# SyncE asks for the experts' first matrix two tiles ahead, in the order in which the slots come free

## The reference

```python
# layer 0: 16 experts, hidden width 512, each token goes to its 2 best
h = relu(einsum('bsh,ehf->bsef', x, w1) + b1)
expert_out = einsum('bsef,efh->bseh', h, w2) + b2
moe = sum over the token's 2 experts of topk_w * expert_out

# layer 1: 8 experts, hidden width 1024, each token goes to its 2 best
xe = xn * ln_g[e] + ln_b[e]
h = gelu(xe @ W1[e] + b1[e])
y = h @ W2[e] + b2[e]
out = sum over the token's 2 experts of weights * y
```

## Time and profile before

| | us |
|---|---|
| three runs of the kernel, median | 3487.85 |
| lowest and highest of them | 3473.99, 3497.01 |
| the profiled execution, its own time | 3479.88 |
| its span, first to last instruction | 3478.1 |
| of it, experts 0 (first hidden to last result) | 1328.4 to 1655.5 |
| of it, experts 1 (first hidden to last result) | 3022.0 to 3456.4 |

### The profile page before, as it was taken

One profiled execution on the slowest core, in us unless ns is written; L12 is line 12 of the kernel. 1 busy time (PEld: TensorE's weight loads), 2 busy tenths in 40 slices (PEclk: granted clock), 3 DMA queues, 4 the chain that ended last, 5 costly groups with the idle time before them and its releaser, 6 DMA issues. The chain is left out here.

```text
span 3478.1 us, 51218 instructions
## 1 busy us (share of the span) xinstructions
PE 2500.1 (72%) x14080; PEld 1914.7 (55%) x14080; DVE 1343.8 (39%) x4118; ACT 1441.6 (41%) x3690; POOL 2011.4 (58%) x1969
## 2 busy tenths in 40 slices
PE   0156899999999947887036666666666667499997
PEld 0123666678888836776024444444444445488986
DVE  4166889952221142000643444444444435500100
ACT  0025666647650022332354444444444443255553
POOL 0353777777777226663657777777777772033332
PEclk9998999999999958998557667666766768699998
DMA  2574766678888335565367777777777772364232
GB/s 112 191 251 126 209 202 206 206 226 257 269 257 244 123 119 186 181 208 171 104 186 203 202 198 202 202 205 204 206 203 201 205 201 61 124 179 131 37 84 62
DMA packets 314743, 620.94 MB, mean 179 GB/s; under 512 B 82206, under 2 KB 128685, under 8 KB 309777
## 3 DMA queue, kind: packets, MB, share of 16 engines
q1 hardware_dynamic: 207409, 343.11, 30.1%
q0 software_dynamic: 101360, 268.76, 29.2%
q10 hardware_dynamic: 5728, 6.11, 0.5%
HBM read 451.74 MB, written 170.90 MB: 179 GB/s over the span
## 5 line engine op out<-in xcount | busy, mean ns | idle before, releaser
L608 POOL DMA_INDIRECT agg_r_rows<-h_table,parts_and_x x856 | 869.1, 1015 | 296.1 <-issue 218.8
L657 PE MATMUL agg_r_sums<-agg_r_rows,agg_r_onehot 128*128 128x257 f32 x1712 | 703.2, 559 | 389.8 <-DVE agg_r_rows L629 343.6
L657 PEld LDWEIGHTS agg_r_sums<-agg_r_rows,agg_r_onehot 128*128 128x128 f32 x1712 | 430.4, 275 | 645.4 <-issue 581.5
L1412 POOL DMA_INDIRECT rl_buf<-r_table,kinds x608 | 634.4, 1043 | 249.3 <-issue 170.4
L629 DVE TENSOR_TENSOR agg_r_rows<-agg_r_rows,agg_r_rel 128x514 f32<-128x514 f32 x428 | 298.5, 697 | 657.6 <-DMA agg_r_rows<-h_table,parts_and_x 655.6
L575 ACT ACTIVATE agg_r_gap<-iota,parts_and_x 128x128 f32<-128x128 f32 x856 | 295.1, 392 | 496.5 <-PE agg_r_sums L657 470.9
L1782 PE MATMUL f_pH<-f_xT,f_w 128*128 128x128 f32 x2816 | 359.4, 287 | 74.5 <-DMA f_w<-in_L_ffn_w 52.9
L1782 PEld LDWEIGHTS f_pH<-f_xT,f_w 128*128 128x128 f32 x2816 | 343.8, 201 | 106.2 <-DMA f_w<-in_L_ffn_w 57.7
L1134 PE MATMUL ly_acc<-parts,matrix 128*128 128x256 bf16 x1250 | 342.0, 274 | 0.0
L1133 PE MATMUL ly_acc<-parts,matrix 128*128 128x256 bf16 x1250 | 340.2, 272 | 0.0
L1132 PE MATMUL ly_acc<-parts,matrix 128*128 128x257 bf16 (+1 forms) x1250 | 340.0, 272 | 0.0
(11 more groups left out here) (394 smaller groups left out, 3404.2 us busy)
## 6 DMA issues: line engine op xcount, KB each, us to landing
agg_r_rel<-relation_rows SPq DMA_DIRECT2D x428, 260.0 KB, 3.0
relation_rows<-rl_buf SPq DMA_DIRECT2D x304, 260.0 KB, 4.5
f_w<-in_L_ffn_W SPq DMA_DIRECT2D x28, 1024.0 KB, 5.0
f_w<-in_L_ffn_w SPq DMA_DIRECT2D x38, 512.0 KB, 5.8
relation_rows<-f_rr_buf POOLq DMA_DIRECT2D x60, 260.0 KB, 2.8
agg_r_rows<-h_table,parts_and_x POOLq DMA_INDIRECT x856, 3.4
ly_zin<-zh SPq DMA_DIRECT2D x50, 256.0 KB, 4.8
zh<-ly_out SPq DMA_DIRECT2D x50, 256.0 KB, 2.7
```

The costliest lines, as they stand in the source:

```text
L608: pool.indirect_dma_start(rows[:, n % SLOTS, t, :], None, table, bass.IndirectOffsetOnAxis(ap=indices[:, t:t + 1], axis=0)).then_inc(s_row ...
L657: last = nc.tensor.matmul(sums[:, n % BANKS, 0:used], onehot[:, n % BANKS, t, :], rows[:, n % SLOTS, t, 0:used], start=t == 0, stop=t == 1)
L1412: pool.indirect_dma_start(self.buf[:, n, g, :], None, self.table, bass.IndirectOffsetOnAxis(ap=self.c.kinds[:, at:at + 1], axis=0)).then_i ...
```

## The change

`tile` is split in three: `first(t, s)` asks for the first matrix of tile t, `second(t, s)` for the second matrix, `stored(i, s)` stores the result of tile 2i + s - 2. SP now runs first(0), first(1), second(0), first(2), second(1), first(3), and then for each tile t: second(t), the store, first(t+2). Since `first` and `second` of one call are for different tiles, each reads the expert and the flag for itself: two more table reads per tile. The waits before each DMA are the same as before.

```diff
-                def tile(i, s, stores):
-                    t = 2 * i + s
+                def first(t, s):
                     e = sp.value_load(e_tab[0:1, 0, bass.ds(t, 1)], min_val=0, max_val=ne - 1)
                     fresh = sp.value_load(e_tab[0:1, 1, bass.ds(t, 1)], min_val=0, max_val=1)
...
                     sp.wait_ge(s_h, t * HB + HB)
-                    weights(sp, fresh, w1b[:, s, :, :].rearrange("p k f -> p (k f)"), a1, s_w1[s])
+                    weights(sp, fresh, w1b[:, s, :, :].rearrange("p k f -> p (k f)"), w1[bass.ds(e, 1), :, :].rearrange("a p f -> p (a f)"), s_w1[s])
+
+                def second(t, s):
+                    e = sp.value_load(e_tab[0:1, 0, bass.ds(t, 1)], min_val=0, max_val=ne - 1)
+                    fresh = sp.value_load(e_tab[0:1, 1, bass.ds(t, 1)], min_val=0, max_val=1)
 
                     sp.wait_ge(s_y, t + 1)
-                    weights(sp, fresh, w2b[:, s, :, :].rearrange("p k f -> p (k f)"), a2, s_w2[s])
-                    if stores and out is None:
-                        sp.wait_ge(s_yb, t + 1)
-                        sp.dma_start(ys[bass.ds((i - 1) * (2 * P) + s * P, P), :], yb[:, s, :]).then_inc(s_st[s], 16)
+                    weights(sp, fresh, w2b[:, s, :, :].rearrange("p k f -> p (k f)"), w2[bass.ds(e, 1), :, :].rearrange("a p f -> p (a f)"), s_w2[s])
+
+                def stored(i, s):
+                    sp.wait_ge(s_yb, 2 * i + s + 1)
+                    sp.dma_start(ys[bass.ds((i - 1) * (2 * P) + s * P, P), :], yb[:, s, :]).then_inc(s_st[s], 16)
...
                 for s in range(2):
-                    tile(0, s, False)
-                with sp.Fori(1, tiles // 2) as i:
+                    first(s, s)
+                for s in range(2):
+                    second(s, s)
+                    first(2 + s, s)
+                with sp.Fori(1, tiles // 2 - 1) as i:
                     for s in range(2):
-                        tile(i, s, True)
+                        second(2 * i + s, s)
+                        if out is None:
+                            stored(i, s)
+                        first(2 * i + 2 + s, s)
+                for s in range(2):
+                    second(tiles - 2 + s, s)
+                    if out is None:
+                        stored(tiles // 2 - 1, s)
```

More of the change, by code:

```diff
@@ L1720, in _ @@
             def _(sp):
-                def tile(i, s, stores):
-                    t = 2 * i + s
+                def first(t, s):
                     e = sp.value_load(e_tab[0:1, 0, bass.ds(t, 1)], min_val=0, max_val=ne - 1)
                     fresh = sp.value_load(e_tab[0:1, 1, bass.ds(t, 1)], min_val=0, max_val=1)
-                    a1 = w1[bass.ds(e, 1), :, :].rearrange("a p f -> p (a f)")
-                    a2 = w2[bass.ds(e, 1), :, :].rearrange("a p f -> p (a f)")
                     sp.wait_ge(s_h, t * HB + HB)
-                    weights(sp, fresh, w1b[:, s, :, :].rearrange("p k f -> p (k f)"), a1, s_w1[s])
+                    weights(sp, fresh, w1b[:, s, :, :].rearrange("p k f -> p (k f)"), w1[bass.ds(e, 1), :, :].rearrange("a p f -> p (a f)"), s_w1[s])
+                def second(t, s):
+                    e = sp.value_load(e_tab[0:1, 0, bass.ds(t, 1)], min_val=0, max_val=ne - 1)
+                    fresh = sp.value_load(e_tab[0:1, 1, bass.ds(t, 1)], min_val=0, max_val=1)
                     sp.wait_ge(s_y, t + 1)
-                    weights(sp, fresh, w2b[:, s, :, :].rearrange("p k f -> p (k f)"), a2, s_w2[s])
-                    if stores and out is None:
-                        sp.wait_ge(s_yb, t + 1)
-                        sp.dma_start(ys[bass.ds((i - 1) * (2 * P) + s * P, P), :], yb[:, s, :]).then_inc(s_st[s], 16)
+                    weights(sp, fresh, w2b[:, s, :, :].rearrange("p k f -> p (k f)"), w2[bass.ds(e, 1), :, :].rearrange("a p f -> p (a f)"), s_w2[s])
+                def stored(i, s):
+                    sp.wait_ge(s_yb, 2 * i + s + 1)
+                    sp.dma_start(ys[bass.ds((i - 1) * (2 * P) + s * P, P), :], yb[:, s, :]).then_inc(s_st[s], 16)
                 for to, what in loads:
```

## The result

The changed kernel takes 3432.97 us (median of 4 runs, 3423.82 to 3436.64). The kernel before, run beside it, takes 3480.92 us (4 runs). The ratio is 0.9856, with a 95% interval of 0.9824 to 0.9887: 48 us less, faster by more than 1%. The profiled execution took 3435.33 us, span 3433.3; before it was 3479.88 and 3478.1, so 44.8 us of span went. 17 us were forecast.

What follows compares the result with a forecast made beforehand. PE's stalls on the first matrix cost time, but SP was to become the pace of experts 0. Gains of 9.1 us in experts 1 and 8 in experts 0 gave 3463 us profiled, 3471 on the median; range 3446 to 3508.

Steps and rivals of the forecast that it cites:

- SP's own work for a tile: Experts 0, before the change: SP's instructions take 3.4 us per tile against PE's 3.91, leaving 0.5 us to spare.
- The price of the reads: Experts 0: the second pair of table reads adds 1.35 us per tile to SP, bounds 1.1 and 1.7.
- the prediction's own chain: Experts 0: SP sets the pace at 4.75 us per tile, 59 tiles 280 us; stage ends at 1647 with crowding.
- The lead: Experts 0: SP's lead of one result and one hidden is used up at 0.8 us per tile after some six tiles.
- its sign of being wrong: Experts 0: hidden still starting 7.82 us apart every two tiles, instead of 9.5, would show the prediction wrong.
- The crowded stretch: Experts 0, tiles 48 to 58, ten of eleven fresh: transfers crowd at 5.5 us per tile; 6 us added, bounds 0 and 25.
- Experts 1: Second experts stage: all eight first-matrix stalls go, 9.7 us, net 9.1 us; added table reads cost nothing there.
- w2(1): Start of experts 0: tile 1's second matrix, asked for at about 1335 instead of 1321, costs at most 1 us.
- Rival one: Experts 0: SP doesn't become the pace, reads being cheaper or overlapping a wait; 82 us go, 3406 us; chance 0.12.
- Rival two: Experts 0, tiles 48 to 58: crowded transfers keep PE at 8 us per tile instead of 5.5; 3492 us; chance 0.10.
- Rival three: Experts 0: PE's pause in every tile lowers TensorE's clock, under 0.76; up to 3522 us at 0.60; chance 0.08.

Runs made afterwards that it cites:

- the split: New order in only one stage, old order in the other, against the kernel before on one chip: experts 0 only 0.9953, experts 1 only 0.9989.

## Why the prediction was wrong in size

**The step that failed** is SP's own work for a tile, taken as 2.7 + 3.1 + 2 x 0.5 over two tiles, 3.4 us each, from the passes of L1713 in the earlier trace rows. The pieces held waits. SP's waits in 1352 to 1433 before, of which the earlier trace rows has only the first line:

```profile
SPq L1735 <- DVE f_yb L1963: 7.3, 21, 0.4
```

7.3 us in 21 waits for DVE's bias, 0.35 us per tile, lie between the second wait of a tile and its store, so inside the pieces of 2.7 and 3.1 us. And the 0.5 us from the first wait to the second, taken as free of waits at the end of the stage, ended as result(58) ended, so SP was waiting for it. The trace of after has no wait of SP in that stretch, and shows the pieces bare. Passes of L1713 from a second wait to the next first wait, then of L1713 and L1717 from that first wait to the following second:

```profile
L1713 SPq EVENT_SEMAPHORE  x2: 17/17/17, 1362.8 to 1365.1; - x2
```

```profile
L1713 SPq EVENT_SEMAPHORE  x2: 17/17/17, 1365.1 to 1366.7; - x2
```

```profile
L1717 SPq EVENT_SEMAPHORE  x2: 17/17/17, 1365.3 to 1367.0; - x2
```

From the second wait over the store and the reads to the first wait: 1362.8 to 1365.1, 2.3 us, not 2.7. From the first wait to the second, now with reads between: 1365.1 to 1366.7, 1.6 us. L1717 comes 0.2 us behind the pass, and the reads follow directly, so without them this piece is about 0.3, not 0.5; the added pair is 1.3 us, as taken (1.35). The price of the reads was right; the base that it was added to was not. The steady rate:

```profile
L1713 SPq EVENT_SEMAPHORE  x35: 17/17/17, 1352.0 to 1423.3; - x35
```

34 steps, 17 tiles, in 71.3 us are 4.19 us per tile, where 4.75 was forecast and 4.5 was the low bound. Without the pair that is 2.9, not 3.4. The waits before say the same: PE's 3.91 less 14.3 / 20 in the earlier trace rows (without the one of 6.5) less 0.35 is 2.85, and 2.85 + 1.3 is 4.2. The text had the 0.7 and let 3.2 pass as agreeing with 3.4. With 4.19 in place of 4.75 the prediction's own chain gives 59 x 0.56 = 33 us less, so the stage would end at 1614 instead of 1647. It ended at 1618.1 after a start 4 us earlier. So this one term explains the miss and overshoots by 8 us; where these 8 us lie is said below.

**The lead** was to be used up after some six tiles at 0.8 us each. At 0.28 us each it lasts longer: hidden starts 3.92 us apart from tile 6 to tile 16 (1350.94, 1390.16) and 4.19 us apart from there to tile 24. So for ten tiles hidden starts 7.84 us apart every two, which the prediction had named as its sign of being wrong, and then 8.38, not 9.5; and PE waits for SP in four tiles, not in nearly every one. Timeline of PE after, start, us, instructions, [idle before, releaser]:

```profile
1350.94 2.02 PE L1794 MATMUL f_pH<-f_xT,f_w 128*128 128x128 f32 x16
...
1390.16 2.02 PE L1794 MATMUL f_pH<-f_xT,f_w 128*128 128x128 f32 x16 [0.16 <-ACT f_xT L1873]
...
1398.68 2.05 PE L1794 MATMUL f_pH<-f_xT,f_w 128*128 128x128 f32 x16 [0.30 <-SPq L1717]
...
1415.12 2.05 PE L1794 MATMUL f_pH<-f_xT,f_w 128*128 128x128 f32 x16 [0.30 <-SPq L1717]
1419.28 2.05 PE L1794 MATMUL f_pH<-f_xT,f_w 128*128 128x128 f32 x16 [0.16 <-SPq L1717]
1423.69 2.02 PE L1794 MATMUL f_pH<-f_xT,f_w 128*128 128x128 f32 x16 [0.41 <-SPq L1717]
1433.37 3.79 PE L1794 MATMUL f_pH<-f_xT,f_w 128*128 128x128 f32 x16 [5.71 <-DMA f_w<-in_L_ffn_w]
```

PE does wait for SP at 1398.68 and from 1415.12 on, in small pieces, as the mechanism says. But the larger price of SP's pace is elsewhere: the last line. The first fresh tile behind the quiet stretch, tile 25, finds no lead. SP's issues there, then the same in the kernel that reads the expert only where fresh:

```profile
1427.74 0.35 SPq L1715 DMA_DIRECT2D f_w<-in_L_ffn_w  x1
```

```profile
1430.05 0.35 SPq L1716 DMA_DIRECT2D f_w<-in_L_ffn_w  x1
```

PE was ready for hidden(25) at 1433.37 - 5.71 = 1427.66, and SP asked for its matrix at 1427.74: the whole landing of 5.6 us is a stall, and hidden(25) then takes 3.79 us. The two lines can't be compared as they stand, since the second execution enters experts 0 8.2 us later: there SP asked at 1430.05, 1.0 us before the start of hidden(24), and hidden(25) started at 1434.95 without a stall; hidden(26) waited 0.31 us. In the changed kernel SP asked 4 us after the start of hidden(24). The same holds for hidden(40): a stall of 5.42 us after (at 1500.81), none with fewer reads, where hidden(41) waited 1.73. That two such stalls stay was not in the prediction, which had the requests far enough ahead in all of the stage.

**The crowded stretch.** The forecast's chain gives 11 x 4.75 us and 0.4 us for each of 20 requests, 60 us or 5.5 per tile, and the 6 us for crowding come on top: 66 us. Measured were 60.3. With 4.19 the chain gives 54, so crowding cost the 6 us that it was given. The other parts miss the same way: hidden(0) to hidden(48) took 212.4 us where the forecast has some 227 (second(46) at 1339.4 + 44 x 4.75 + some 4 for fresh tiles, hidden(48) 3 us later), and the rest of the stage 21.0 where it has 25. With 4.19 the first of these becomes some 203, and that is where the 8 us of the overshoot lie: the two stalls before tiles 25 and 40, with a slow hidden behind each, were in no term of the sum.

**Experts 1.** All eight stalls went, as forecast; 7.7 us against 9.1. ACT's tokens are late next, and the added reads are under cover, as said.

**w2(1)**, asked for later, cost nothing that shows: PE's first wait for a second matrix is 0.62 us, at 1341.36, a tile later.

**Rival one** (3406 us, SP not the pace) stands nearer to the measured time, by 27 us against 38, but only because the kernel before ran 7 us lower beside the result. In the gain, its 82 us are 34 off the measured 48, and the forecast's 17 are 31 off. Its reason is wrong: SP is the pace of experts 0, only narrowly, and in the crowded stretch the transfers cost time as well. The kernel that takes reads away shows how far its reason reaches: 57.7 us less than before on its chip, not 82. **Rival two** (crowded transfers stay at 8 us per tile) is refuted by 5.5; its share of 0.70 did have room up to 0.92. **Rival three** (the clock falls, to under 0.76 in the stage) is refuted: the granted clock was 0.97 over the stage, and 1.00 in 1350 to 1395 and in 1536 to 1597, where pauses of 0.9 to 2.4 us before hidden left it at 2.05 us. But short pauses can bring the clock down. When the changed kernel ran again on a chip of the same kind, two of them did, and the crowded stretch had 0.94; timeline of PE and the stretch:

```profile
1542.69 3.52 PE L1794 MATMUL f_pH<-f_xT,f_w 128*128 128x128 f32 x16 [2.25 <-DMA f_w<-in_L_ffn_w]
...
1576.71 3.42 PE L1794 MATMUL f_pH<-f_xT,f_w 128*128 128x128 f32 x16 [1.95 <-DMA f_w<-in_L_ffn_w]
```

```profile
1542.00:1603.00 61.00, 47.73 (x285) 41.41 (x286) 4.25 (x10) 16.88 (x66) 32.78 (x38) 0.94 0.91 293
```

The Trainium skill's rule that was weighed, "TensorE: Matmul & The Clock Gate", section "A second HAM failure mode: psum-queue depth-cycling", by which frequent short pauses between groups of matmuls make the clock swing, so has something to it here: such dips occur in some executions. They are too few to move the stage, which had 0.97 in that run as well. The Trainium skill's rule of "DMA: Bandwidth & Descriptors", section "Rules for kernel authors", to issue a transfer early, gave the sign of this change rightly, and the reading that the early request is paid with sequencer time holds too: the changed kernel gains 48 us and leaves 12 more to whoever shortens SP's work.

## What to carry to other kernels

A piece of a sequencer's time read off the distance of two passes may hold a wait: list every wait of that engine in the stretch, of every line, and take them all off before something is added to the rest. Where an engine's work and its pace come within some tenths of a microsecond per tile, give the forecast as both cases, since 59 tiles turn 0.56 us into 33. After an order of requests is changed, look at what the issuing engine does per tile: here two reads of a table that most tiles don't need were worth a quarter of the gain again.

## What was not expected of the hardware

The same program takes 3430 to 3480 us on some chips and 3990 to 4070 on others, with the same count of instructions and nearly the same busy time of PE (2492.0 and 2514.1 us in the changed kernel). A large part of the difference is in idle pieces that the profile puts down to no releaser ("issue"). Waits of PE in the changed kernel on such a chip, first the largest over the whole span, then in experts 0; then in experts 0 of the version with fewer reads and no relation rows on another of that kind:

```profile
PE agg_r_sums L657 <- issue: 296.6, 78, 22.7
```

```profile
PE f_pH L1794 <- issue: 39.2, 33, 1.7
```

```profile
PE f_pH L1793 <- issue: 1.1, 3, 0.6
```

On the chip of the result neither of these rows is there. With POOL's gathers and their stores left out beside the tiles, the pieces all but go in experts 0 (the fewer reads alone leave 22.6 us of them on that chip), so POOL's gathers or the traffic of the DMA engines have a part in them; what an engine lacks in these moments stays open. SP's tile is longer there too, 5.13 us against 4.19. In the total the change was worth less on such a chip, 27 us against 48, though experts 0 and experts 1 gained 32.3 and 10.9 us in the profiles of the split; why the totals show less isn't known.

A second thing: the DMA engines reached a busy share of 0.92 and 291 GB/s over 61 us. That the crowd of requests would lengthen each landing was the fear behind rival two. Issues of the crowded stretch after, with the median us to landing:

```profile
f_w<-in_L_ffn_w SPq DMA_DIRECT2D x19, 512.0 KB, 5.6
```

In the same stretch of the kernel before, with the engines 0.65 busy, it was 5.9 us in 17 issues. The crowd does show against the rest of the stage, 4.5 us in 12 issues in 1340 to 1534 after; but asking for more in less time made it no worse.
